# Closing layer 0's rounds with 32x32 block turns, and measuring half of the features inside layer 1's block

## The chip, the cores and the metric

The kernel runs on one core of a Trainium2 chip. The metric is the time of one execution on the device in microseconds. The core has five engines that run side by side, each with its own queue of instructions: TensorE (PE, with its weight load as PEld), VectorE (DVE), ScalarE (ACT), GpSimd (POOL) and SyncE (SP, which issues DMAs). They are ordered by semaphores alone. TensorE's clock has two levels, 1.2 and 2.4 GHz; the profile gives the granted clock as a share of the upper one.

## The reference

The input is x (2048 nodes x 256 features) and an adjacency matrix (2048 x 2048). Four layers follow each other, each of the form x = layernorm(x + layer(x)):

- Layer 0: attention with 8 heads of 32 over the neighbours. For each head, scores q k^T / sqrt(32), masked by the adjacency, softmax, times v.
- Layer 1: a graph attention layer. Wh = x W^T; e = leaky_relu(s_dst + s_src), masked, softmax, times Wh, which gives h_prime (2048 x 256). Then each *feature* is normalised over the 2048 nodes: `gamma * (h_prime - mean) * rsqrt(var + eps) + beta`, and relu.
- Layer 2: the mean over at most the first 64 neighbours of each node (a cumulative count along the row says which are kept), two projections with leaky relu.
- Layer 3: the mean over all neighbours, projections, relu.

## The kernel before

The program is one function after another, each with a block in which the five engines have their own instruction lists; at the end of a block all engines meet. `attention` is layer 0 and prepares for the next. `general_attention` follows it: a slow, exact way that runs only if a flag `doubt` says that a softmax sum was too small; in this run it is skipped, but every engine loads the flag and branches there. `layer1` computes h_prime; another `general_attention` follows, then `tail`, with the feature norm, layers 2 and 3.

**Layer 0** (`attention`). The work is laid out transposed: for a block of 512 destination nodes and a group of 4 heads, 16 tiles of 128 source nodes are gone through in 8 steps of two tiles. That is a *round*; there are 8 rounds, 64 steps (`STEPS`). In step s and for head h, TensorE makes scores for 2 x 512 (`score`, L340 and the mask added by L344) into one of three PSUM buffers; ScalarE takes the exponential (L484) into `ex`; VectorE adds it to a running sum `esum` (L555). After every second step TensorE multiplies two steps' `ex` by v into `mixed_ps` (`mix`, L359), in the order scores of step s, then mix of s-2 and s-1. At a round's end VectorE halves the sum (`halve`, L561), and TensorE sums over the partitions with a matrix of ones (`total`, L378, in the last round L370), so that `total_ps` has, for each of 4 heads, 32 equal rows of 512 totals. In the first half (steps below 32) ScalarE also turns the raw adjacency of coming tiles into marks of 8 bits (`convert`, L450, two at the end of each even step), and SyncE loads the raw tiles two steps ahead (L207). On some steps ScalarE and VectorE split inputs into a high and a low part (L441, L503).

The round is closed by VectorE in the next round, by `keep(it, piece)`, one piece behind each of its sums in steps 1 to 3 of that round (after the loop, all pieces for the last round): piece 0 copies `mixed_ps` to `yT` (L569, then `stored`, for which the next `mix` waits); 1 takes the maximum of the totals and a tiny number (L572); 2 finds the smallest total (L575, L577); 3 to 6 take the reciprocal in four parts of 128 (L581); 7 multiplies `yT` by it (L585); 8 adds the residual (L589), which SyncE loads after the totals (L217). After the last round a small matmul (`count_fine`, L98) and L659 make `doubt`.

**Layer 1** (`layer1`). Head by head, VectorE and ScalarE make masks and TensorE multiplies (L997 and L1004) into 8 PSUM banks, `acc`: banks 0 to 3 for the first half of the nodes, 4 to 7 for the second. VectorE joins the pieces of a half (`join_pieces`, L1121) and weighs them (`finish`). In the last head's loop `divide` writes h_prime for heads 0 to 6 (L1139); `finish_last` does the last head. Behind the main loop TensorE begins layer 2's cumulative count in banks 0 to 3 (class `Cumulation`): per tile t of 128 sources, `up_to_source` (L1715), `compare` on ScalarE with a sigmoid (L1729), and `cumulate` (L1721), each in 4 pieces of 512. These pass a tile to and fro between TensorE and ScalarE. Tiles 0 and 1 (`AHEAD`) are done in this block, then L98 and L1157 make `doubt`.

**The tail** (`tail`). SyncE loads gamma and beta. TensorE turns the first 128 features (k = 0) of h_prime with 16 transposes into banks 4 to 7 (L1364); VectorE measures them (`feature_stats`, four L1515 and L1517); GpSimd takes the root (L1650, L1652); VectorE makes the factors (L1521, L1524, L1527); ScalarE applies them with a relu into `hpT`, in two halves (L1464). Then the same for k = 1, turned into the same banks. Meanwhile the comparison goes on: tile 2 stands ahead of the first application on ScalarE, tiles 3 to 5 behind it, then the second application; from tile 6 on each step s of the loop has one comparison beside back turns, layer norm and projections of layer 2.

The order of all this is written out by hand, in each engine's list. The lines that the change touches lie in `attention` (`keep`, `sum_weights`, the loops of ScalarE and VectorE), `general_attention`, `layer1` (`finish_last` and the ends of the lists) and `tail`.

## Time and profile before

| | |
|---|---|
| median of 3 runs | 869.05 us (868.21 to 869.98) |
| the profiled execution's own time | 870.34 us |
| its span, first to last instruction | 868.6 us |
| mean granted clock of TensorE | 0.988 |
| TensorE busy | 810.2 us (93%) |
| VectorE busy | 691.6 us (80%) |
| ScalarE busy | 568.3 us (65%) |
| GpSimd busy | 148.5 us (17%) |
| layer 0 (span time) | 0 to 409 us |
| layer 1 | 409 to 644 us |
| tail | 644 to 868.6 us |

Times of rows are microseconds from the span's start. TensorE's matmuls overlap, so a busy TensorE is not one at its peak; a group that is named with x16 is a run of 16 instructions, and its time goes from the first's start to the last's end. An arrow `<-` in brackets says what an engine had waited for before the row.

### The profile page before, as it was taken

To read this page: it belongs to the slowest core of one execution; us is meant where nothing else is said; L and a number is where in the kernel's file an instruction comes from. 1 tells how busy PE (TensorE), PEld (TensorE's weight loads), DVE (VectorE), ACT (ScalarE), POOL (GpSimd) and SP (SyncE) were. 2 spreads that over 40 slices of the span, in tenths; PEclk is the share of its full clock that TensorE was granted. 3 is DMA by queue.
4 is the path that set the end of the run, shared out by engine and by line. 5 is a ranking of instruction groups with operands and counts; after the bars stand their busy time and mean duration, and the time that the engine had idled before them with its cause. 6 is when DMAs were issued, how large, how long until landed. Compare 5 with 4: busy or idle time off the path is not lost. (4 is left out here: it accounts for less than half of the span.)

```text
span 868.6 us, 18889 instructions
## 1 busy us (share of the span) xinstructions
PE 810.2 (93%) x7820; PEld 507.0 (58%) x7820; DVE 691.6 (80%) x1053; ACT 568.3 (65%) x568; POOL 148.5 (17%) x287
## 2 busy tenths in 40 slices
PE   3899999999999999995869999999968999999997
PEld 1334444333444434342559999999943557777786
DVE  6686989899998989897789999999943585555444
ACT  6798989897777767672369999999848630111000
POOL 2511011753110010000420000000001352111122
PEclk9999999999999999998999999999999999999999
DMA  8965344393302020001221111111000000000011
GB/s 291 263 197 169 110 137 144 95 246 85 99 16 58 1 61 1 14 1 37 85 86 52 51 32 48 32 48 48 3 1 1 1 1 1 1 1 1 2 49 49
DMA packets 28615, 56.85 MB, mean 65 GB/s; under 512 B 5808, under 2 KB 10032, under 8 KB 27120
## 3 DMA queue, kind: packets, MB, share of 16 engines
q1 hardware_dynamic: 24400, 46.19, 17.2%
q0 software_dynamic: 4128, 9.44, 4.1%
q8 instruction: 62, 1.02, 0.5%
q14 instruction: 25, 0.20, 0.1%
HBM read 38.70 MB, written 2.23 MB: 47 GB/s over the span
## 5 line engine op out<-in xcount | busy, mean ns | idle before, releaser
L484 ACT ACTIVATE ex<-scores_ps,shift 128x1024 f32<-128x1024 f32 x256 | 262.4, 1129 | 77.7 <-PE scores_ps L344 69.9
L555 DVE TENSOR_TENSOR esum<-esum,ex 128x1024 f32<-128x1024 f32 x192 | 222.9, 1211 | 7.1 <-ACT ex L484 7.1
L340 PE MATMUL scores_ps<-qst,kst 128*128 128x512 f32 x512 | 201.3, 474 | 2.9 <-ACT ex L484 2.2
L997 PE MATMUL banks<-fx,pos 128*128 128x132 f16 x2048 | 160.3, 221 | 7.1 <-DVE pos L1174 6.8
L1267 ACT ACTIVATE steps<-a_all,big_b_head 128x2048 fp8e5<-128x2048 f32 x86 | 163.6, 1988 | 0.0
L344 PE MATMUL scores_ps<-edge,negI 128*128 128x512 fp8e5 x512 | 155.3, 385 | 0.0
L340 PEld LDWEIGHTS scores_ps<-qst,kst 128*128 128x128 f32 x512 | 89.8, 189 | 70.9 <-ACT ex L484 19.8
L997 PEld LDWEIGHTS banks<-fx,pos 128*128 128x128 fp8e5 x2048 | 121.3, 98 | 8.0 <-issue 6.5
L1004 PE MATMUL banks<-fm,edge 128*128 128x66 f16 x2048 | 104.1, 193 | 0.0
L1004 PEld LDWEIGHTS banks<-fm,edge 128*128 128x128 fp8e5 x2048 | 86.6, 98 | 0.0
L1174 DVE TENSOR_TENSOR pos<-steps,edge 128x1024 int32<-128x1024 int32 (+1 forms) x65 | 77.4, 1202 | 2.4 <-PE banks L997 2.2
L344 PEld LDWEIGHTS scores_ps<-edge,negI 128*128 128x128 bf16 x512 | 29.7, 99 | 70.1 <-issue 70.1
L555 DVE TENSOR_TENSOR esum<-ex 128x1024 f32<-128x1024 f32 x32 | 38.9, 1221 | 32.8 <-ACT ex L484 32.5
L1394 PE MATMUL banks<-w,xT_ring 128*128 128x512 f32 x128 | 60.4, 594 | 0.7 <-DVE own L1558 0.6
L359 PE MATMUL mixed_total_ps<-ex,cur 128*32 128x512 f32 x512 | 58.2, 595 | 0.0
L359 PE MATMUL mixed_total_ps<-ex,v 128*32 128x512 f32 x512 | 58.2, 595 | 0.0
L1407 PE MATMUL banks<-y_halves_second,edge 128*128 128x256 f16 x512 | 56.7, 273 | 0.5 <-DVE y_halves_second L1552 0.5
L1407 PEld LDWEIGHTS banks<-y_halves_second,edge 128*128 128x128 fp8e5 x512 | 50.0, 98 | 8.7 <-issue 2.3
L284 POOL DMA_DIRECT2D qst<-high_low x56 | 27.6, 503 | 159.7 <-PE scores_ps L344 138.8
L1407 PE MATMUL banks<-y_halves,kept_rest 128*128 128x256 f16 x448 | 52.0, 273 | 0.5 <-DVE y_halves L1552 0.5
L1164 DVE TENSOR_SCALAR steps<-a_all,negb 128x2048 fp8e5<-128x2048 f32 x40 | 50.5, 1281 | 0.6 <-DMA a_all<-score_rows_dram 0.6
L1477 ACT COPY xT_ring<-banks 128x256 f32<-128x256 f32 x32 | 11.9, 371 | 57.1 <-PE banks L1383 56.8
(210 smaller groups left out, 915.5 us busy)
## 6 DMA issues: line engine op xcount, KB each, us to landing
adj_raw<-in_adjT_dram SPq DMA_DIRECT2D x32, 512.0 KB, 5.5
a_all<-score_rows_dram SPq DMA_DIRECT2D x7, 1024.0 KB, 4.7
kst<-high_low SPq DMA_DIRECT2D x56, 64.0 KB, 4.5
kst<-high_low POOLq DMA_DIRECT2D x56, 64.0 KB, 5.0
qst<-high_low POOLq DMA_DIRECT2D x56, 64.0 KB, 2.2
qst<-high_low SPq DMA_DIRECT2D x56, 64.0 KB, 3.7
ex<-in_x2T_dram SPq DMA_DIRECT2D x2, 1024.0 KB, 6.9
ex<-in_xT_dram SPq DMA_DIRECT2D x2, 1024.0 KB, 8.9
```

What stands on the lines that cost most here:

```text
L340: nc.tensor.matmul(to, kst[:, h, jt * P:(jt + 1) * P], qst[:, it % 2, h, :], start=True, stop=False)
L344: last = nc.tensor.matmul(to, negI[:], edge[:, jt, columns(it % NC)], start=False, stop=True)
L359: last = nc.tensor.matmul(mixed_ps[h * DH:(h + 1) * DH, :], (v0, v1)[it // NC][:, jt, h * DH:(h + 1) * DH], ex[:, s % ER, h, t * CW:(t + 1 ...
L484: nc.scalar.activation(ex[:, s % ER, h, :], scores_ps[:, u % SR, :], ACT.Exp, bias=shift[:, it // NC * HG + h:it // NC * HG + h + 1], scal ...
L555: nc.vector.tensor_tensor(esum[:, h, :], other, ex[:, s % ER, h, :], ALU.add).then_inc(summed, 1)
L997: done = nc.tensor.matmul(place(half, i), pos[:, group_of(h, k, half) % GR, jt % GU, i * P:(i + 1) * P], fx[:, e, jt].rearrange("p k r c - ...
L1004: done = nc.tensor.matmul(place(half, i)[:, C:2 * C], edge[:, jt, at:at + P], fm[:, e, jt].rearrange("p r c -> p (r c)"), start=False, sto ...
L1164: nc.vector.tensor_scalar(steps[:, pair_of(h, k) % SLOTS, jt % GU, :], aall[:, h % 2, :], negb[:, jt, one(h)], MARK, ALU.is_gt, ALU.mult, ...
L1174: nc.vector.tensor_tensor(pos[:, group_of(h, k, half) % GR, first:end, :].bitcast(int32), steps[:, pair_of(h, k) % SLOTS, first:end, at].b ...
L1267: nc.scalar.activation(steps[:, pair_of(h, k) % SLOTS, jt % GU, :], aall[:, e, :], ACT.Relu, bias=bigh[:, e, jt:jt + 1], scale=BIG, satura ...
L1394: last = nc.tensor.matmul(proj_ps[:, t % 2, :], xT[:, t % 2, k, :], (w2, w3)[layer][:, k, :], start=(k == 0), stop=(k == KT - 1))
L1407: last = nc.tensor.matmul(nb_ps[:, t % 2, 0:D], which, halves[layer][:, jt, r, :], start=(jt == 0 and r == 0), stop=(jt == T - 1 and r == 1))
```

## The change

In **layer 0** `keep` becomes `close`, with 5 pieces in place of 9. The copy of `mixed_ps` goes to ScalarE (`keep_mixed`), in step 0 of the next round behind the fourth exponential and ahead of the conversions, where it waits for the round's last mix. The totals, 32 equal rows per head, are turned in 32x32 blocks by VectorE (piece 0), so that each partition has 16 distinct values in one column of each block; maximum, minimum and reciprocal run on these 16 (piece 1); a second turn of the 16, spread over 32 each, gives the rows back (piece 2). Pieces 3 and 4 are the multiplication and the residual.

In **layer 1** gamma and beta are loaded; TensorE turns the first half of the features (k = 0), which `divide` has finished, into banks 0 to 3 behind the main loop, the last bank first, and VectorE measures them in `finish_last`; the cumulative count moves to banks 4 to 7 and behind these turns, and waits for the second half's join as well. `count_fine` writes to a column of the last feature bank, behind the first tile's cumulation; that column's tile is turned once more at the end. The general way turns and measures them anew if it runs.

In the **tail** the first steps are now the root and the factors of k = 0. Tile 2's comparison stands behind the first application. The PSUM banks 0 to 3 and 4 to 7 change places.

```diff
@@ attention
-    PIECES = 4
+    CLOSING = 4
-        recip, res = half_sum[:, 0, :], half_sum[:, 1, :]
+        recip, res, turned = half_sum[:, 0, :], half_sum[:, 1, :], half_sum[:, 2, :]
+        compact = S.sb("distinct_sums", [P, CW // DH], fp32)
@@ sum_weights (tensor)
-                    pe.wait_ge(recip_step, (s // JP - 1) * (PIECES + 1) + 1)
+                    pe.wait_ge(recip_step, (s // JP - 1) * CLOSING + 1)
@@ scalar
+                def keep_mixed(it):
+                    act.wait_ge(mixed, (it + 1) * JP)
+                    nc.scalar.copy(yT[:, it // NC, columns(it % NC)], mixed_ps).then_inc(stored, 1)
...
+                        if jp == 0 and it and h == HG - 1:
+                            keep_mixed(it - 1)
...
+                keep_mixed(ROUNDS - 1)
@@ vector
-                def keep(it, piece):
...
+                def close(it, piece):
+                    g, at, done = it // NC, columns(it % NC), it * CLOSING
                     if piece == 0:
-                        dve.wait_ge(mixed, (it + 1) * JP)
-                        nc.vector.tensor_copy(yT[:, g, at], mixed_ps).then_inc(stored, 1)
+                        dve.wait_ge(totals, it + 1)
+                        nc.vector.transpose(turned, total_ps).then_inc(recip_step, 1)
                     elif piece == 1:
-                        dve.wait_ge(totals, it + 1)
-                        nc.vector.tensor_scalar(recip, total_ps, TRUST / 2, None, ALU.max).then_inc(recip_step, 1)
-                    elif piece == 2:
-                        dve.wait_ge(recip_step, it * (PIECES + 1) + 1)
-                        nc.vector.tensor_reduce(out=least[:], in_=recip, axis=AX.X, op=ALU.min).then_inc(lowest, 1)
+                        dve.wait_ge(recip_step, done + 1)
+                        nc.vector.tensor_scalar(compact[:], turned.rearrange("p (b r) -> p b r", r=DH)[:, :, 0], TRUST / 2, None,
+                                                ALU.max).then_inc(recip_step, 1)
+                        dve.wait_ge(recip_step, done + 2)
+                        nc.vector.tensor_reduce(out=least[:], in_=compact[:], axis=AX.X, op=ALU.min).then_inc(lowest, 1)
                         dve.wait_ge(lowest, it * 2 + 1)
                         nc.vector.tensor_tensor(low, least[:], low, ALU.min).then_inc(lowest, 1)
-                        dve.wait_ge(lowest, it * 2 + 2)
-                    elif piece < 3 + PIECES:
-                        part = slice((piece - 3) * CW // PIECES, (piece - 2) * CW // PIECES)
-                        nc.vector.reciprocal(recip[:, part], recip[:, part]).then_inc(recip_step, 1)
+                        nc.vector.reciprocal(compact[:], compact[:]).then_inc(recip_step, 1)
+                    elif piece == 2:
+                        dve.wait_ge(recip_step, done + 3)
+                        nc.vector.transpose(recip, compact[:].unsqueeze(2).broadcast_to([P, CW // DH, DH])).then_inc(recip_step, 1)
@@ general_attention, layer 1 only
+                    if layer:
+                        pe.wait_ge(result_ready, U)
+                        pe.wait_ge(returned, 16)
+                        for b in range(NC):
+                            feature.turn(0, b).then_inc(summed, 1)
@@ layer1
+        cum_ps = acc[:, NC:2 * NC, :]
                 sp.wait_ge(pair_landed, there)
+                feature.load(sp, gamma, beta)
@@ tensor
                 pe.wait_ge(evac, LAST * 2 + 1 + EV0)
+                pe.wait_ge(heads_made, 1)
+                for b in feature.order(0):
+                    feature.turn(0, b).then_inc(feature.turned, 1)
+                pe.wait_ge(evac, LAST * 2 + 2 + EV0)
                 pe.wait_ge(count.consts, 3)
                 for c in range(NC):
-                    count.up_to_source(acc, 0, c)
+                    count.up_to_source(cum_ps, 0, c)
                 for t in range(count.AHEAD):
-                    count.cumulate(pe, acc, t)
-                count_fine(pe, nc, fine_made, ones, fine, acc[:, 7, 0:1], counted)
+                    count.cumulate(pe, cum_ps, t)
+                    if t == 0:
+                        pe.wait_ge(feature.stats, 1)
+                        count_fine(pe, nc, fine_made, ones, fine, feature.ps[:, NC - 1, 0:1], counted)
+                pe.wait_ge(counted, 2)
+                feature.turn(0, NC - 1, 1)
@@ finish_last (vector)
                     nc.vector.tensor_scalar(fine[:], low, MARK * SURE, None, ALU.is_ge).then_inc(fine_made, 1)
+                    feature.take_stats(dve, 0)
@@ tail
-        turn_hp = ps[:, NC:2 * NC, :]
-        cum_ps = ps[:, 0:NC, :]
+        cum_ps = ps[:, NC:2 * NC, :]
@@ tensor
                 for b in range(NC):
-                    turn_features(0, b)
-                count.cumulate(pe, cum_ps, count.AHEAD)
-                for b in range(NC):
-                    turn_features(1, b)
-                for t in range(count.AHEAD + 1, LEAD):
+                    if b % 2 == 0:
+                        pe.wait_ge(applied, b // 2 + 1)
+                    feature.turn(1, b).then_inc(feature.turned, 1)
+                for t in range(count.AHEAD, LEAD):
                     count.cumulate(pe, cum_ps, t)
@@ scalar
-                count.compare(act, cum_ps, count.AHEAD)
                 for half in range(2):
                     apply(0, half)
-                for t in range(count.AHEAD + 1, LEAD):
+                for t in range(count.AHEAD, LEAD):
                     count.compare(act, cum_ps, t)
@@ vector
-                feature_stats(0)
-                dve.wait_ge(gb_landed, 16 * (1 + KT))
-                feature_factors(0)
-                feature_stats(1)
-                feature_factors(1)
+                feature.factors(dve, 0)
+                feature.take_stats(dve, 1)
+                feature.factors(dve, 1)
@@ new: class FeatureNorm (load, take_stats, find_root and factors as in the tail before)
+    def load(self, sp, gamma, beta):
+        sp.dma_start(self.gcol[:], gamma).then_inc(self.landed, 16)
+        for k in range(KT):
+            sp.dma_start(self.bcol[:, k:k + 1], beta[k * P:(k + 1) * P].rearrange("(p o) -> p o", o=1)
+                         ).then_inc(self.landed, 16)
+        sp.wait_ge(self.landed, 16 * (1 + KT))
+
+    def order(self, k):
+        return range(NC) if k else (NC - 1, *range(NC - 1))
+
+    def turn(self, k, b, count=NC):
+        for t in range(NC * b, NC * b + count):
+            last = self.nc.tensor.transpose(self.ps[:, b, t % NC * P:(t % NC + 1) * P],
+                                            self.hp[:, t, k * P:(k + 1) * P], self.ident[:])
+        return last
```

## Rows read from the trace of the kernel before

**Rows 1.** Busy time by stretch: PE, PEld, DVE, ACT, POOL, PEclk, DMA share, GB/s.

```profile
350.00:398.00 48.00, 47.22 (x289) 18.78 (x287) 44.52 (x49) 32.27 (x32) 0.00 (x0) 1.00 0.02 6
644.50:712.00 67.50, 60.38 (x270) 29.84 (x270) 39.38 (x115) 46.36 (x65) 22.55 (x45) 1.00 0.01 1
```

**Rows 2.** Timeline of ScalarE at round boundaries (start us, us, ...).

```profile
120.46 2.23 ACT L450 ACTIVATE edge<-adj_raw,twos 128x1024 fp8e5<-128x1024 int32 x2
124.42 8.14 ACT L484 ACTIVATE ex<-scores_ps,shift 128x1024 f32<-128x1024 f32 x8 [1.73 <-PE scores_ps L344]
...
357.87 8.15 ACT L484 ACTIVATE ex<-scores_ps,shift 128x1024 f32<-128x1024 f32 x8 [4.16 <-PE scores_ps L344]
```

**Rows 3.** Timeline of TensorE at the boundary of 124 us.

```profile
118.77 3.64 PE L359 MATMUL mixed_total_ps<-ex,cur 128*32 128x512 f32 x32
...
129.60 0.73 PE L340 MATMUL scores_ps<-qst,kst 128*128 128x512 f32 x2
```

**Rows 4.** Groups by line and form, 60 to 400 us; last, the waits.

```profile
L581 DVE RECIPROCAL half_sum<-half_sum 128x128 f32<-128x128 f32 x28 | 26.4, 942 | 0.0
...
L441 ACT CAST high_low<-natural 128x512 fp32r<-128x512 f32 x9 | 5.6, 620 | 0.0
L569 DVE COPY cur<-mixed_total_ps 128x512 f32<-128x512 f32 x8 | 5.5, 684 | 0.0
...
PE mixed_total_ps L378 <- DVE half_sum L561: 0.7, 3, 0.3
```

**Rows 5.** Timeline of layer 0's end; last, the DMA issues (KB, us to landing).

```profile
391.11 4.13 ACT L484 ACTIVATE ex<-scores_ps,shift 128x1024 f32<-128x1024 f32 x4 [2.93 <-PE scores_ps L344]
...
393.74 3.64 PE L359 MATMUL mixed_total_ps<-ex,v 128*32 128x512 f32 x32
...
398.80 1.92 PE L370 MATMUL mixed_total_ps<-esum,ones 128*32 128x512 f32 x16 [1.42 <-DVE esum L555]
...
402.51 3.38 DVE L581 RECIPROCAL half_sum<-half_sum 128x128 f32<-128x128 f32 x4
...
406.64 0.69 DVE L589 TENSOR_TENSOR cur<-cur,half_sum 128x512 f32<-128x512 f32 x1
...
half_sum<-in_xT_dram SPq DMA_DIRECT2D x1, 256.0 KB, 3.1
```

**Rows 6.** Timeline of the end of layer 1's block.

```profile
633.68 1.02 PE L1715 MATMUL banks<-edge,before_in_tile 128*128 128x512 fp8e5 x4
...
634.36 1.28 ACT L1729 ACT_TABLE_LOAD   x1 [8.53 <-PE banks L1715]
...
635.65 2.12 ACT L1729 ACTIVATE kept_head<-banks,limit 128x1024 fp8e5<-128x1024 f32 x2
...
640.39 1.11 ACT L1729 ACTIVATE kept_head<-banks,limit 128x1024 fp8e5<-128x1024 f32 x1 [0.59 <-PE banks L1715]
...
642.75 0.16 DVE L1157 TENSOR_SCALAR doubt<-banks 128x1 int32<-128x1 f32 x1 [4.78 <-PE banks L98]
```

**Rows 7.** Timeline of the tail's first 17 us.

```profile
644.56 1.94 PE L1364 MATMUL banks<-ident,cur 128*128 128x128 f32 x16 [1.85 <-PEq L696]
...
647.75 0.26 DVE L1517 BATCH_NORM_AGGREGATE feature_mean_var<-feature_stats 128x2 f32<-128x24 f32 x1
...
649.65 2.30 ACT L1464 ACTIVATE hp_turned<-banks,feature_scale_shift 128x1024 f32<-128x1024 f32 x2 [1.66 <-DVE feature_scale_shift L1527]
...
654.15 2.12 ACT L1729 ACTIVATE kept_rest<-banks,limit 128x1024 fp8e5<-128x1024 f32 x2 [0.18 <-PE banks L1715]
...
660.65 2.12 ACT L1729 ACTIVATE kept_rest<-banks,limit 128x1024 fp8e5<-128x1024 f32 x2
```

**Rows 8.** Busy time by stretch (columns as in rows 1), with the granted clock.

```profile
638.50:640.30 1.80, 1.80 (x6) 0.59 (x5) 0.00 (x0) 1.11 (x1) 0.00 (x0) 0.50 0.00 0
```

**Rows 9.** Timeline of ScalarE, the first table load.

```profile
0.80 1.28 ACT L441 ACT_TABLE_LOAD   x1 [0.80 <-PEq L1906]
5.67 0.62 ACT L441 CAST high_low<-ex 128x512 fp32r<-128x512 f32 x1 [3.59 <-DMA ex<-in_x2T_dram]
```

More of the change, by code:

```diff
@@ L640, in _ @@
                         piece = (jp - 1) * HG + h
-                        if it and 0 <= piece <= 4 + PIECES:
-                            keep(it - 1, piece)
+                        if it and 0 <= piece <= CLOSING:
+                            close(it - 1, piece)
                         if W_AT + 2 <= s < W_AT + 4:
@@ L807, in _ @@
                             nc.vector.tensor_tensor(to[:, g, :], to[:, g, :], (sc, pT)[g][:], ALU.add)
+                    else:
+                        dve.wait_ge(summed, U + NC)
+                        step = Chain(dve, chain, U * STEPS)
+                        for b in range(NC):
+                            step(nc.vector.bn_stats(feature.st[:, 0, b, :], feature.ps[:, b, :]))
+                        nc.vector.bn_aggr(feature.mv[:, 0, :], feature.st[:, 0].rearrange("p b s -> p (b s)"))
 def layer1(nc, S, w, ident, ones, mhalf, yT, x1, edge, wh1, score_rows, fac, efac, negb, bigb, sums, low, fine, doubt,
-           hp, pair, count, sources, ps):
+           hp, pair, count, sources, ps, feature, gamma, beta):
     TG = 4
@@ L1298, in _, with tail @@
                 for t in range(count.AHEAD):
-                    count.compare(act, acc, t)
-def tail(nc, S, gamma, beta, ident, ones, mhalf, hp, cur, edge, w2, bias2, w3, bias3, eps1, scale, count, ps, out):
+                    count.compare(act, cum_ps, t)
+def tail(nc, S, ident, ones, mhalf, hp, cur, edge, w2, bias2, w3, bias3, scale, count, ps, feature, out):
     xn = cur[:, :].rearrange("p (t d) -> p t d", d=D)
@@ L1348, in _ @@
             def _(sp):
-                sp.dma_start(gcol[:], gamma).then_inc(gb_landed, 16)
-                for k in range(KT):
-                    sp.dma_start(bcol[:, k:k + 1], beta[k * P:(k + 1) * P].rearrange("(p o) -> p o", o=1)
-                                 ).then_inc(gb_landed, 16)
                 for t in range(0, T, TD):
@@ L1359, in _ @@
             def _(pe):
-                def turn_features(k, b):
-                    if k:
-                        pe.wait_ge(applied, b // 2 + 1)
-                    for t in range(NC * b, NC * (b + 1)):
-                        last = nc.tensor.transpose(turn_hp[:, b, t % NC * P:(t % NC + 1) * P],
-                                                   hp[:, t, k * P:(k + 1) * P], ident[:])
-                    last.then_inc(hp_turned, 1)
                 def back(t):
@@ L1648, in _ @@
                 for k in range(KT):
[L1649 to L1652 removed]
+                    feature.find_root(pool, k)
                 def root(n):
@@ L1879, in gat_layer @@
         layer1(nc, S, w, ident, ones, mhalf, yT, x1, edge, wh1, score_rows, fac, efac, negb, bigb, sums, low[:, 1:2], fine,
-               doubt[:, 1:2], hp, pair, count, sources, banks)
-        general_attention(nc, S, 1, doubt[:, 1:2], ident, (score_rows, wh1), adj, scratch1, hp, banks)
+               doubt[:, 1:2], hp, pair, count, sources, banks, feature, gamma, beta)
+        general_attention(nc, S, 1, doubt[:, 1:2], ident, (score_rows, wh1), adj, scratch1, hp, banks, feature)
 def kernel(x, adj, L0_gnn_x2, L0_gnn_v, L1_gnn_W, L1_gnn_a, L1_gnn_gamma, L1_gnn_beta, L2_gnn_W_nb, L2_gnn_b_nb,
```

114 lines of the change are left out of this document (59 added, 55 removed).

## The prediction

> **What bounds the kernel now.** Start with the busy time by stretch: in the second half of layer 0 TensorE works 47.22 of 48 us, VectorE 44.52, ScalarE 32.27; in the tail's first 67.5 us TensorE has 60.38, VectorE only 39.38 [rows 1]. Work taken from VectorE is worth something only where TensorE waits for it. So read next, one engine at a time, the two places where the engines wait for each other: a round boundary of layer 0, and the two block ends (layer 0, layer 1) where everything drains. The list of waits in the stretch 60 to 398 us shows 0.7 us in all of TensorE waiting for VectorE's half sums [rows 4]: VectorE's reciprocals in the rounds are covered. ScalarE is not free in the first four rounds: it also converts adjacency tiles, and waits only 1.73 us at the boundary at 124.42, against 4.16 us in a late round [rows 2].
>
> **Layer 0, ScalarE takes the copy of the mixed values.** The copy waits for the last mixing matmul of the round, and behind it in ScalarE's queue stand two conversions (2.23 us) and the exponentials of the next step. The mixing of the boundary shown ends at 118.77 + 3.64 = 122.41 [rows 3]; the conversions ran meanwhile, from 120.46 [rows 2]. Now they come after: 122.41 + 0.05 of latency, a copy of 128x512 (as the cast of that shape, 0.62, of which 0.1 overlaps the next instruction [rows 4]) to 122.98, conversions to 125.1, where the next exponential began at 124.42 [rows 2]: 0.7 us late. Is there slack? TensorE's eighth score of the pair of steps starts at 129.60 [rows 3] and needs the fifth exponential, which ends at 124.42 + 5 x 1.02 = 129.5 (1.02 is 8.14 / 8 [rows 2]). No slack is left, so TensorE is shifted by the 0.7, for good. Conversions stand at three boundaries (steps 8, 16, 24): **+2.1 us**. Bounds: 0 if something absorbs it, 3 x 1.0. At the four later ones the copy lies in an idle time of 4.16 us [rows 2], from after the mixing on: free. The adjacency loads are issued 0.7 us later and still two steps ahead of use; I take nothing for them.
>
> **Layer 0, VectorE.** Per round go a copy, a maximum and a minimum over 512 (0.68 each) and four reciprocals of 0.94 [rows 4], 5.8 us in all; two turns and three operations on 16 elements come. The trace shows no turn on VectorE. The nearest row is the copy of the same 512 columns out of PSUM, 0.68 [rows 4], and I take that, since both stream the tile once; the ends are a free turn and the reciprocal's pace, 4 x 0.94 = 3.8. The Trainium skill, VectorE: DVE Perf Modes, The three transpose paths, gives 311 ns for a 128x128 bf16 turn; four of them would be an estimated 1.24 us, and the sum below would end 1.1 us higher (two turns). A small operation costs between 0.16 (one element [rows 6]) and 0.94; I take 0.2. So 2 x 0.68 + 3 x 0.2 = 2.0 us replace 5.8, and VectorE gains 3.8 per round. In the rounds that buys the 0.7 us of waits [rows 4]: **-0.7 us**.
>
> At the end of layer 0 it buys more. TensorE's mixing ends at 393.74 + 3.64 = 397.38, but the totals start at 398.80, 1.42 us late, behind VectorE's last sum [rows 5]. ScalarE had given the last exponential at 391.11 + 4.13 = 395.24 [rows 5], so the last sum could end at 395.24 + 1.2 = 396.4, before the mixing does. VectorE is late by its backlog of 2.3 us, and 3.8 removes it: **-1.4 us**. What is late next is the mixing. Then all of the closing work is bare: out go 3.38 us of reciprocals [rows 5] and two passes of 0.68 [rows 4], 4.7 in all, in come 2.0 and some issue gaps of 0.1: **-2.6 us**. Its last step is the residual sum at 406.64 [rows 5]; the residual is loaded after the totals, 3.1 us to landing [rows 5], and is needed about 3.2 us after them now. That just fits; what is saved beyond this would be lost to it. (The final copy on ScalarE lies beside the totals; its cover is their 1.92 us.)
>
> **End of layer 1.** TensorE's first cumulating matmuls start at 633.68 [rows 6], right behind the main loop. Now 16 turns stand before them; the same 16 took 1.94 us in the tail [rows 7]. The wait for the second half's pieces, joined in the meantime, adds none. ScalarE's table load and all that follows are that much later: **+1.9 us**. VectorE's statistics (at most the 3.4 us from 644.56 to their end at 648.01 [rows 7]) come while ScalarE and TensorE pass the tiles to and fro, ahead of doubt, for which VectorE had waited 4.78 us [rows 6]: free, and so is the retaken single turn (a sixteenth of 1.94). The three small loads of gamma and beta now stand on SyncE's queue, with a wait for their landing, ahead of head 1's row; even 3.1 us as for the residual [rows 5] each lies beside head 0, an eighth of the main loop: nothing. Dropping them from the tail brings nothing either, the factors came after them.
>
> **The tail.** From its first instruction at 644.56 to the comparison of tile 6 at 660.65 are 16.1 us [rows 7]. In it ScalarE had room: it loaded its table and compared tile 2 in the shadow of the first half's turns, statistics and root. Now the chain is: root and factors, 649.65 - (647.75 + 0.26) = 1.64 us; two applications, 2.2 (2.30 less overlap); comparisons of tiles 2 to 5 at 2.12 + 0.18 each, 9.2, less a last 0.18; two applications, 2.2 [rows 7]. That is 15.1. A table load comes on top. The tail's first activation is now a Relu and no longer a sigmoid, so the sigmoid's table load (1.28 us, and 0.01 after it the activation starts [rows 6]) comes behind the applications, unhidden. A load ahead of the Relu, if there is one, stands before that activation's wait, as the one at 0.80 does [rows 9], and is over within the 1.64. Sum 16.3: **+0.2 us**. So 3.4 us of turning and measuring leave the chain, and a comparison of 2.3 and a load of 1.28 enter it. The Trainium skill, ScalarE: Activation LUTs, What ACT_TABLE_LOAD costs, puts a switch at 2.66 us with its drain; by that the sum would be 1.4 higher.
>
> **Sum.** +2.1 - 0.7 - 1.4 - 2.6 + 1.9 + 0.2 = -0.5 us against the profiled execution, whose own time is 870.34, 1.3 above the median of 869.05. Applied to the median: 868.6. A measurement of this kernel can tell 0.2%, 1.7 us, from no change.
>
> **The rivals.** (a) *The boundaries cost nothing*: some slack takes up ScalarE's 0.7, three times; -2.6 us, **866.5**. For it: TensorE waits little there. Against: row 129.60 fits ScalarE to 0.1 us. Chance 0.15. (b) *The clock stays up at the end of layer 1*: behind an idle TensorE (from 634.70 until half of the first comparison was done, 635.65 + 1.06: 2.0 us [rows 6]), the granted clock was 0.50 [rows 8] (1.2 of 2.4 GHz), and from the table load's end at 635.64 to the last comparison's end at 641.50 went 5.86 us [rows 6], where the tail's pace, 2.30 + 2.12, would make it 4.42. If the turns ahead keep the clock up, -1.4 more: **867.1**, chance 0.15. (c) *Slower, the clock falls in the tail*: TensorE now rests from the end of layer 1's block until the first application has ended, 1.6 us between the blocks (642.91 to 644.56 [rows 6, 7]), 1.64 and half of 2.3, 4.4 in all, longer than the 2.0 us before the row of 0.50. The difference in (b), 1.4 us, is what one tile's matmuls at half rate cost. On the forecast's -0.5, it decides from two such tiles on: +2.8, **871.4**. For: that row. Against: the fall comes not after every rest (1.85 us before 644.56 left the turns at full pace [rows 7]), and half rate over the turns alone is partly covered by the table load. Chance 0.15. (d) *A turn costs two passes*, 2 x 0.68, one to fill and one to empty its block, between the bounds: +1.4, **870.0**; or the table load holds ScalarE for two of its rows, 1.3 more, against [rows 6], which show 0.01 behind it: 869.9. Together 0.08. The two estimates from the Trainium skill above, each cited there with its page, come to about these. (e) *VectorE's backlog doesn't go*, so that the change does not do what it says at the end: the 1.4 stays, **870.0**, chance 0.05. The forecast itself, 868.6, has the remaining 0.42.
>
> **How the numbers follow.** Forecast, (d) and (e) lie within 0.2% of 869.05: 0.55. Faster: (a), (b) 0.30, the likelier small misses of the forecast on that side counted in them. Slower: (c), 0.15. The range runs from just below (a) up to (c) with two tiles, and leaves out three tiles, a turn at the reciprocal's pace, and (a) with (b): 866.0 to 871.4.
>
> **What would show it.** In the changed profile: a copy on ScalarE before the conversions at 124 us and the exponential after them 0.7 us later, the eighth score with it; the totals at layer 0's end starting with the mixing's end, and 2.7 us less from there to the last sum; the turn's row at 0.7 us; the first cumulating matmul 1.9 us behind the main loop; in the tail a table load between application and comparison, and 16.3 us to the comparison of tile 6. The prediction is wrong if the conversions stay in the mixing's shadow, if a turn takes over 1.3 us, or if the tail's granted clock is 0.5 over more than one tile.

## Result, and the profile after

| | before | after |
|---|---|---|
| median of the runs made together | 869.0 us (866.8 to 869.98, 5 runs) | 865.03 us (864.0 to 866.28, 5 runs) |
| ratio, 95% interval | | 0.9957 [0.9943, 0.9972] |
| the profiled execution's own time | 870.34 us | 866.28 us |
| its span, mean granted clock | 868.6 us, 0.988 | 864.4 us, 0.985 |

The kernel is faster by 4.0 us, 0.43%. The prediction said 868.6, from 866.0 to 871.4: too little gain, and the result lies below its range. Busy time of the changed kernel, from its page:

```profile
PE 813.0 (94%) x7821; PEld 510.5 (59%) x7821; DVE 665.1 (77%) x1037; ACT 574.2 (66%) x577; POOL 132.3 (15%) x287
```

VectorE has lost 26.5 us. The second half of layer 0, to be set beside [rows 1] (PE, PEld, DVE, ACT, POOL, clock, DMA share, GB/s):

```profile
350.00:398.00 48.00, 47.26 (x298) 18.76 (x296) 39.23 (x45) 31.98 (x33) 0.00 (x0) 1.00 0.02 6
```

TensorE is as busy there as before, with VectorE 5.3 us lighter. The gain is not in these shares, but in single waits. Layer 0 as the changed kernel's timeline has it, first ScalarE and TensorE at the boundary of [rows 2, 3]:

```profile
122.09 0.59 ACT L456 COPY cur<-mixed_total_ps 128x512 f32<-128x512 f32 x1 [1.85 <-PE mixed_total_ps L360]
122.58 2.19 ACT L451 ACTIVATE edge<-adj_raw,twos 128x1024 fp8e5<-128x1024 int32 x2
124.67 2.11 ACT L489 ACTIVATE ex<-scores_ps,shift 128x1024 f32<-128x1024 f32 x2
...
118.39 3.64 PE L360 MATMUL mixed_total_ps<-ex,cur 128*32 128x512 f32 x32
121.84 1.04 PE L379 MATMUL mixed_total_ps<-half_sum,ones 128*32 128x512 f32 x8
```

The copy waits for the mixing, the conversions come behind it, and the exponential follows at 124.67 with no idle time, 6.28 us after the mixing's start; in [rows 2, 3] it was 124.42 - 118.77 = 5.65. So each of the three boundaries costs 0.62. VectorE's closing work in the next steps:

```profile
126.94 0.71 DVE L576 STREAM_TRANSPOSE half_sum<-mixed_total_ps 128x512 f32<-128x512 f32 x1
127.58 1.18 DVE L563 TENSOR_TENSOR esum<-ex 128x1024 f32<-128x1024 f32 x1
128.68 0.17 DVE L579 TENSOR_SCALAR distinct_sums<-half_sum 128x16 f32<-128x16 f32 x1
128.88 0.17 DVE L582 TENSOR_REDUCE least_sum<-distinct_sums 128x1 f32<-128x16 f32 x1
129.09 0.16 DVE L584 TENSOR_TENSOR lowest_sums<-least_sum,lowest_sums 128x1 f32<-128x1 f32 x1
129.16 0.25 DVE L585 RECIPROCAL distinct_sums<-distinct_sums 128x16 f32<-128x16 f32 x1
129.32 1.16 DVE L563 TENSOR_TENSOR esum<-ex 128x1024 f32<-128x1024 f32 x1
130.40 0.70 DVE L588 STREAM_TRANSPOSE half_sum<-distinct_sums 128x512 f32<-128x512 f32 x1
```

A turn of 128x512 f32 takes 0.71, whether it reads PSUM or spreads 16 columns: the duration of the copy it was priced by. By the Trainium skill, VectorE: DVE Perf Modes, The three transpose paths, it would have been an estimated 1.24; these rows decide. The end of layer 0, TensorE and then VectorE, to be set beside [rows 5]:

```profile
391.91 3.64 PE L360 MATMUL mixed_total_ps<-ex,v 128*32 128x512 f32 x32
395.37 1.90 PE L371 MATMUL mixed_total_ps<-esum,ones 128*32 128x512 f32 x16
...
403.19 0.66 PE L966 MATMUL banks<-ident,cur 128*128 128x128 f32 x2 [3.91 <-PEq L706]
...
397.33 0.72 DVE L576 STREAM_TRANSPOSE half_sum<-mixed_total_ps 128x512 f32<-128x512 f32 x1 [2.28 <-PE mixed_total_ps L371]
...
400.56 0.69 DVE L596 TENSOR_TENSOR cur<-cur,half_sum 128x512 f32<-128x512 f32 x1 [0.20 <-DMA half_sum<-in_xT_dram]
```

The totals now follow the mixing at once, and from their start to the last sum are 5.19 us, where there were 7.84. The end of layer 1 and the tail's start, TensorE and then ScalarE, beside [rows 6, 7]:

```profile
627.84 1.94 PE L1748 MATMUL banks<-ident,cur 128*128 128x128 f32 x16
629.61 1.03 PE L1703 MATMUL banks<-edge,before_in_tile 128*128 128x512 fp8e5 x4
...
642.98 3.53 PE L1748 MATMUL banks<-ident,cur 128*128 128x128 f32 x16 [4.35 <-ACT hp_turned L1476]
...
630.29 1.28 ACT L1717 ACT_TABLE_LOAD   x1 [10.31 <-PE banks L1703]
...
640.21 1.28 ACT L1476 ACT_TABLE_LOAD   x1 [2.79 <-PEq L706]
641.72 2.30 ACT L1476 ACTIVATE hp_turned<-banks,feature_scale_shift 128x1024 f32<-128x1024 f32 x2 [0.22 <-DVE feature_scale_shift L1772]
644.04 1.28 ACT L1717 ACT_TABLE_LOAD   x1
645.33 2.12 ACT L1717 ACTIVATE kept_rest<-banks,limit 128x1024 fp8e5<-128x1024 f32 x2
...
656.46 2.13 ACT L1717 ACTIVATE kept_rest<-banks,limit 128x1024 fp8e5<-128x1024 f32 x2
```

The turns put the first cumulating matmul 1.77 us behind the main loop; the tail has two table loads, the first hidden behind the root, the second not. TensorE's clock fell to its lower level over the turns of the second half of the features (busy time by stretch, columns as in [rows 1]; the clock is the third number from the end):

```profile
642.98:646.50 3.52, 3.52 (x16) 3.13 (x17) 2.10 (x3) 3.49 (x4) 0.00 (x0) 0.53 0.02 5
```

Behind an idle time of 4.35 they took 3.53 us, not 2.19 as in kernels where they follow 1.82 of idle. The cover is the table load and tile 2's comparison: tile 3's comparison waited only 0.21 for TensorE.

### The profile page after: what moved, and what is told of

It reads as the page before. It is cut to its first block and busy times, and to the rows that moved or that the text cites. A ratio compares the mean times of both kernels' runs of the same rounds, so it can differ in the third digit from the quotient of the medians.

```text
span 864.4 us, 18885 instructions
## 1 busy us (share of the span) xinstructions
PE 813.0 (94%) x7821; PEld 510.5 (59%) x7821; DVE 665.1 (77%) x1037; ACT 574.2 (66%) x577; POOL 132.3 (15%) x287
## 3 DMA queue, kind: packets, MB, share of 16 engines
q0 software_dynamic: 4128, 9.44, 4.4%
q8 instruction: 63, 1.03, 0.5%
## 5 line engine op out<-in xcount | busy, mean ns | idle before, releaser
L563 DVE TENSOR_TENSOR esum<-esum,ex 128x1024 f32<-128x1024 f32 x192 | 223.3, 1219 | 18.1 <-ACT ex L489 17.9
L360 PE MATMUL mixed_total_ps<-ex,cur 128*32 128x512 f32 x512 | 58.2, 595 | 0.0
L360 PE MATMUL mixed_total_ps<-ex,v 128*32 128x512 f32 x512 | 58.2, 595 | 0.0
```

Of the source, the lines that this page charges most:

```text
L360: last = nc.tensor.matmul(mixed_ps[h * DH:(h + 1) * DH, :], (v0, v1)[it // NC][:, jt, h * DH:(h + 1) * DH], ex[:, s % ER, h, t * CW:(t + 1 ...
L563: nc.vector.tensor_tensor(esum[:, h, :], other, ex[:, s % ER, h, :], ALU.add).then_inc(summed, 1)
```

## Where the 4.2 us of the span come from

I followed the start of each mixing (L359, L360 after) through layer 0 in both traces, then the marks of the rows above. Change against the trace of before, step by step:

| step | predicted | measured |
|---|---|---|
| up to the second mixing | 0 | -1.03 |
| three boundaries with conversions | +2.1 | +1.86 |
| step 28, within a round | 0 | +0.13 |
| rounds from step 32 on: half sums | -0.7 | -0.49 -0.32 -0.44 -0.36 = -1.61 |
| weights' sums (L386) in step 38 | 0 | -1.29 |
| totals behind the last mixing | -1.4 | 5.06 - 3.46 = -1.60 |
| closing work to the last sum | -2.6 | -2.65 |
| to layer 1's first matmul | 0 | -0.24 |
| layer 1 | 0 | +0.48 |
| turns ahead of the count | +1.9 | +1.77 |
| comparisons of tiles 0, 1 and block end | 0 | -0.30 |
| tail up to tile 6 | +0.2 | +0.18 |

With 0.1 of rounding along the mixings this is the -4.2 of the span; behind tile 6 both kernels take 207.9 us. Three rows make the miss: the start, the half sums and the weights' sums. The +0.13 is not the copy's: at 182.22 a conversion had waited 0.98 for its adjacency tile's DMA, and experiment 1's trace, with the same list, has 0.00 there. Layer 1's loop took from 223.3 to 224.9 us over the traces of this study, in no order of the edits, so +0.48 is scatter.

The weights' sums stand in the trace of before, TensorE and VectorE, though I hadn't read them:

```profile
246.88 3.64 PE L359 MATMUL mixed_total_ps<-ex,v 128*32 128x512 f32 x32
251.75 1.19 PE L386 MATMUL mixed_total_ps<-w,ones 128*128 128x272 f32 x4 [1.23 <-DVE w L601]
...
250.15 1.22 DVE L555 TENSOR_TENSOR esum<-esum,ex 128x1024 f32<-128x1024 f32 x1
251.28 0.41 DVE L601 TENSOR_REDUCE w<-adj_raw 128x8 f32<-128x256 f32 x1
```

and the changed kernel's:

```profile
247.41 3.64 PE L360 MATMUL mixed_total_ps<-ex,v 128*32 128x512 f32 x32
250.98 1.18 PE L387 MATMUL mixed_total_ps<-w,ones 128*128 128x272 f32 x4
...
248.26 0.41 DVE L608 TENSOR_REDUCE w<-adj_raw 128x8 f32<-128x256 f32 x1
```

VectorE, without its reciprocals, ends the last reduction 3 us earlier, and TensorE goes from the mixing to the sums with no wait. The same list of waits from which [rows 4] took 0.7 has these lines for the kernel before (us in total, times, longest):

```profile
PEld mixed_total_ps L378 <- DVE half_sum L561: 4.9, 5, 1.2
PEld mixed_total_ps L386 <- DVE w L601: 2.1, 1, 2.1
PE mixed_total_ps L386 <- DVE w L601: 1.2, 1, 1.2
```

The list of the changed kernel has none of them. The half sums show why the idle time of PE is too small a price for such a wait:

```profile
355.65 1.06 PE L378 MATMUL mixed_total_ps<-half_sum,ones 128*32 128x512 f32 x8 [0.16 <-DVE half_sum L561]
```

The mixing before it had started at 351.85, 3.80 earlier; where nothing waits the distance is 121.84 - 118.39 = 3.45, less than the mixing's own 3.64, since the next group overlaps it. So a row of 0.16 idle costs 0.35, and the ones of 0.29 and 0.24 (at 215.16 and 310.09) cost 0.49 and 0.44. The totals at 263.93 show no idle time at all, and cost 0.32.

## The experiments

All ratios are against the kernel before, run beside each group of kernels: 869.08 us for experiments 1 to 4, 868.39 for 5 to 8 (made on another chip), 868.94 for 9 to 11. The changed kernel's own 865.03 stood beside 869.0. So kernels of different groups are compared by their ratios, of which 0.001 is 0.9 us.

**1. Layer 0's part alone**: `attention` of the changed kernel, all else of the one before.

> Only the change in layer 0, the feature norm as before. Theory A (the traces laid side by side): layer 0 gave 6.3 us up to the start of layer 1, of which 1.0 stood already before the first round was closed and may be scatter; the features cost 2.1. Then this alone is 5.3 to 6.3 us below before, some 863. Theory B (the prediction's own sum for layer 0, -2.6, with the rest scatter): 2.6 below, 866.4. Theory C (the gain comes from the features after all): within 1 us of before.

Measured: 863.52 us (861.94 to 865.59), ratio 0.9932 [0.9917, 0.9948]. Its steps in layer 0 are those of the changed kernel, save the 0.13. This part alone brings more than the whole change.

**2. The features' part alone**: `attention` of before, the rest changed.

> Only the features turned and measured in layer 1's block, layer 0 as before. Theory A: the turns put the first cumulating matmul 1.8 us behind the main loop and the tail takes 0.2 longer to the comparison of tile 6: 2 us above before, 871. Theory C: 2 us or more below before.

Measured: 871.51 us (868.79 to 873.48), ratio 1.002 [1.0006, 1.0034]. In its trace no step of layer 0 differs from before by over 0.02, except +0.28 at the first mixing and -0.57 at the second, of which experiment 11 tells. The two parts give, by their ratios, -5.9 and +1.7 us, -4.2 in all, against 4.0 measured for the whole change. The prediction had -2.6 and +2.1. So the miss lies in layer 0; the features part costs what it was said to cost.

**3. The copy behind the conversions**, in the changed kernel:

```diff
@@ scalar, attention
-                        if jp == 0 and it and h == HG - 1:
-                            keep_mixed(it - 1)
...
                             convert(s + AHEAD + 1)
+                        if jp == 0 and it and h == HG - 1:
+                            keep_mixed(it - 1)
```

> The changed kernel, with ScalarE's copy of the mixed values behind the two conversions and not ahead of them. Theory A: each of the three early boundaries is 0.62 us late through the order alone, so 1.9 us below the changed kernel, 863.1, and the exponential at 124 us starts 0.87 behind its score's wait as before. Rival: the copy itself is the 0.6, wherever it stands: no change against the changed kernel.

Measured: 863.6 us (861.47 to 865.19), ratio 0.9933 [0.9918, 0.9948]. The three steps of +0.62 are gone (within 0.01), and all others of layer 0 stay; at the boundary the exponential now waits 1.25 for its score, so the copy lies in idle time. The medians differ by 1.4 of the 1.9 that these steps show. The end of layer 1 came out 1.4 shorter in this trace than in the changed kernel's, though nothing was changed there; experiment 6 tells why.

**4. VectorE's load put back**: four reciprocals of 128x128 in each of rounds 1 to 7, on a slice that nobody reads meanwhile (the last halving of the next round waits for them).

```diff
@@ vector, attention
+                        if it and CLOSING < piece <= CLOSING + 4:
+                            n = piece - CLOSING - 1
+                            part = half_sum[:, 3, n * P:(n + 1) * P]
+                            nc.vector.reciprocal(part, part).then_inc(filled, 1)
```

> The changed kernel with four reciprocals of 128x128 put back on VectorE in each of rounds 1 to 7, on half sums that nothing reads any more, so that VectorE is as loaded as before but the closing at layer 0's end stays short. Theory A (VectorE's backlog was what TensorE waited for, at five boundaries, at the weights' column sums and at the last totals): 1.6 + 1.3 + 1.5 = 4.4 us come back, some 869.4. Rival (the prediction: 0.7 + 1.4): 2.1 come back, 867.1.

Measured: 867.9 us (867.09 to 870.3), ratio 0.9989 [0.9976, 1.0001]: 2.9 us of the gain are gone, between the rival's 2.1 and theory A's 4.4. Waits for VectorE are back (list of waits, as above; last, TensorE's timeline at layer 0's end):

```profile
PEld mixed_total_ps L379 <- DVE half_sum L573: 3.7, 5, 1.0
PEld mixed_total_ps L387 <- DVE w L612: 1.8, 1, 1.8
PE mixed_total_ps L387 <- DVE w L612: 0.9, 1, 0.9
...
398.11 1.92 PE L371 MATMUL mixed_total_ps<-esum,ones 128*32 128x512 f32 x16 [1.06 <-DVE esum L565]
```

The totals stand 398.11 - 393.40 = 4.71 behind the last mixing's start, so 1.25 of their 1.60 are back. The step at the weights' sums is -0.36, not -1.29: 0.93 back. The half sums' are -0.30, 0, -0.35, -0.36, so only 0.6 of their 1.6 are back, most of it at one place. That makes 2.8 us, the 2.9 of the medians. What stayed away fits the load: VectorE still has 0.3 us less to do in a round than before (from the first sum of round 4 to its closing work's end 236.24 - 219.18 = 17.06, before 235.87 - 218.53 = 17.34), and 0.30 to 0.36 are missing at five of the six places. So the reciprocals' load brings back most of the waits at the weights' sums and at the last totals, one half sum's in full and another's in part. That the other two belong to it as well is argued from the size of this rest, and from their going with the turns in experiments 1 and 9.

**5. A sigmoid of one column ahead of the tail's first application**, so that the sigmoid's table is loaded in the shadow of the root.

```diff
@@ scalar, tail
+                nc.scalar.activation(warm[:], mhalf[:, 0:1], ACT.Sigmoid)
                 for half in range(2):
                     apply(0, half)
```

> The changed kernel with one sigmoid of a single column ahead of the first application in the tail. Theory A: the sigmoid's table (which serves the relu too) is then loaded in the 1.6 us in which ScalarE waits for the factors, and the second load behind the applications (1.28 us, at 644.04) is gone: 1.2 us less from the tail's first instruction to the comparison of tile 6, 863.8. Rival: TensorE's turns at half clock (3.53 us, to 646.5) end the wait for tile 2's cumulation whatever ScalarE does: then only some 0.2 us of it are gained.

Measured: 865.59 us (864.01 to 867.0), ratio 0.9966 [0.9955, 0.9978]: no gain. Its tail, ScalarE and TensorE:

```profile
641.87 2.31 ACT L1477 ACTIVATE hp_turned<-banks,feature_scale_shift 128x1024 f32<-128x1024 f32 x2
644.06 2.12 ACT L1719 ACTIVATE kept_rest<-banks,limit 128x1024 fp8e5<-128x1024 f32 x2
647.72 2.12 ACT L1719 ACTIVATE kept_rest<-banks,limit 128x1024 fp8e5<-128x1024 f32 x2 [1.54 <-PE banks L1705]
...
643.12 3.16 PE L1750 MATMUL banks<-ident,cur 128*128 128x128 f32 x16 [4.36 <-ACT hp_turned L1477]
646.08 0.63 PE L1711 MATMUL banks<-edge,after_in_tile 128*128 128x512 fp8e5 x1
```

The second load is gone and tile 2's comparison comes 1.4 us earlier, counted from the tail's start, but tile 2's cumulation stands behind the turns at the lower clock, and tile 3 waits 1.54 for it. Load and turns are two covers of nearly the same length; taking away one shows the other. The tail's 16.2 us stay (640.36 to 656.53).

**6. Tile 0's count ahead of the turns**: the count back in banks 0 to 3, the features in 4 to 7.

```diff
@@ tensor, layer1
+                pe.wait_ge(count.consts, 3)
+                for c in range(NC):
+                    count.up_to_source(cum_ps, 0, c)
                 pe.wait_ge(heads_made, 1)
+                pe.wait_ge(evac, LAST * 2 + 2 + EV0)
                 for b in feature.order(0):
                     feature.turn(0, b).then_inc(feature.turned, 1)
-                pe.wait_ge(evac, LAST * 2 + 2 + EV0)
-                pe.wait_ge(count.consts, 3)
-                for c in range(NC):
-                    count.up_to_source(cum_ps, 0, c)
```

> The changed kernel with tile 0's first cumulating matmuls ahead of the feature turns at the end of layer 1's block (the count in banks 0 to 3 and the features in banks 4 to 7, as the tail had them before). Theory A: the 1.8 us by which the turns delayed the count come back, and since TensorE is busy with the turns while ScalarE loads its table and compares tile 0, the granted clock stays up there, which gives another 1.4: 2.5 to 3.2 us less, 862. Rival (the clock falls all the same): 1.4 to 1.8 less, 863.4.

Measured: 862.54 us (862.32 to 863.27), ratio 0.9937 [0.9924, 0.995]. By the ratios that is 1.7 us below the changed kernel (0.9957), which does not exclude the rival. TensorE, and ScalarE's second comparison:

```profile
627.56 1.02 PE L1703 MATMUL banks<-edge,before_in_tile 128*128 128x512 fp8e5 x4
629.16 1.94 PE L1748 MATMUL banks<-ident,cur 128*128 128x128 f32 x16 [0.58 <-DVE part L1152]
630.93 0.38 PE L1709 MATMUL banks<-edge,after_in_tile 128*128 128x512 fp8e5 x1
...
632.06 2.12 ACT L1717 ACTIVATE kept_head<-banks,limit 128x1024 fp8e5<-128x1024 f32 x2 [0.41 <-PE banks L1703]
```

The turns now fill the time in which TensorE had waited for ScalarE, its idle time there shrinks to 0.58, and the cumulating matmuls behind it take 0.38, the pace of the upper clock, not 0.63. From the end of the main loop to the tail's start are 636.97 - 627.56 = 9.41 us, where the changed kernel has 640.21 - 627.84 = 12.37 and the one before 644.58 - 633.68 = 10.90. It is tempting to read this as the turns' 1.77 back and 1.2 of what the lower clock costs. But in the trace of experiment 9, whose list at this place is the changed kernel's, the same matmuls ran at the upper clock too, behind the same idle time of 2.11 (first the changed kernel, then experiment 9):

```profile
632.75 0.47 PE L1709 MATMUL banks<-edge,after_in_tile 128*128 128x512 fp8e5 x1 [2.11 <-ACT kept_head L1717]
633.02 0.63 PE L1703 MATMUL banks<-edge,before_in_tile 128*128 128x512 fp8e5 x1
...
630.50 0.39 PE L1708 MATMUL banks<-edge,after_in_tile 128*128 128x512 fp8e5 x1 [2.11 <-ACT kept_head L1716]
630.72 0.38 PE L1702 MATMUL banks<-edge,before_in_tile 128*128 128x512 fp8e5 x1
```

All traces side by side, from the main loop's end to the tail's start in us:

| order at the end of layer 1 | the clock fell there | the clock stayed up |
|---|---|---|
| count, no turns | 10.90, 10.47, 10.76 (before, experiments 11, 7) | 9.45 (experiment 1) |
| turns, then count | 12.37, 12.50, 12.19 (changed, experiments 2, 5) | 10.96, 10.96, 10.98 (experiments 3, 4, 9) |
| tile 0's count, then turns | | 9.41, 9.42, 9.44 (experiments 6, 8, 10) |

At a like clock the turns ahead of the count cost 1.5 to 1.6 us, and the turns behind tile 0's first matmuls cost nothing. The clock costs another 1.0 to 1.5, and it differs between traces of one and the same list. That it stayed up in the three traces of the last row may be the order's doing or chance; three traces don't show it. In the tail the clock falls in this order too, and its 16.2 us to tile 6 stay (653.19 - 636.97).

**7. Layer 0's part with the copy behind the conversions**, nothing of the features (edits 1 and 3).

> Only the change in layer 0, with the copy behind the conversions. Theory A: the two effects add: 1.5 to 1.9 us less than the layer 0 part alone (863.5), some 861.8.

Measured: 860.27 us (859.67 to 861.03), ratio 0.991 [0.9896, 0.9923]. By the ratios it is 1.9 us below experiment 1 (0.9932), as theory A had it, and 4.1 below the changed kernel. It is the lowest median of all, but experiments 8 and 10 can't be told from it.

**8. All three edits** (3, 5 and 6) in the changed kernel.

> The changed kernel with all three edits: the copy behind the conversions, the sigmoid first, tile 0's matmuls ahead of the turns. Theory A: they add: 865.0 - 1.5 - 1.2 - 2.8 = 859.5, below the layer 0 part alone with its copy behind, so that the feature part, put this way, is a gain. Rival (the features are no gain in any order): 861.8 or above.

Measured: 860.7 us (859.62 to 862.32), ratio 0.9912 [0.9898, 0.9925]. Measuring the features early, in this order, is no loss any more, and no gain over experiment 7 either. From the main loop's end to the tail's start it takes 9.42 us against experiment 7's 10.76, but that is the clock: experiment 1, with experiment 7's list there, took 9.45 with the clock up. The trace was taken of the slowest of the five executions (862.32): TensorE's clock falls over the tail's turns, tile 3's comparison waits 2.41 for TensorE, and the clock falls a second time behind tile 6:

```profile
652.00:655.80 3.80, 3.61 (x10) 1.49 (x11) 0.00 (x0) 2.25 (x3) 0.58 (x2) 0.55 0.00 0
```

In experiment 7's trace the clock of this stretch is 1.00.

**9. The copy left on VectorE**, the turns kept.

```diff
@@ vector, attention, close, piece 0
+                        dve.wait_ge(mixed, (it + 1) * JP)
+                        nc.vector.tensor_copy(yT[:, g, at], mixed_ps).then_inc(stored, 1)
                         dve.wait_ge(totals, it + 1)
                         nc.vector.transpose(turned, total_ps).then_inc(recip_step, 1)
```

> The changed kernel, in which VectorE keeps the copy of the mixed values (ahead of its wait for the totals, in the same piece), so that only the turns distinguish its rounds from before. Theory A (the gain of the rounds comes from the turns, and the copy on ScalarE brought nothing but the three boundaries): the steps of +0.62 us at steps 8, 16 and 24 are gone; VectorE has 0.68 more in each round, still 3.4 less than before, which keeps most of the steps of 0.3 to 0.5 at steps 32 to 56 and at least 0.7 of the 1.29 at the weights' sums; at the end of layer 0 the totals start no more than 0.3 later than in the changed kernel. Median 863 to 864.5, near that of the version with the copy behind the conversions (863.6). Rival B (VectorE stands just at a threshold, and the copy is what brought it under): most of the steps at 32 to 56 and at the weights' sums go, as with the four reciprocals put back: 866 to 868.

Measured: 862.7 us (862.13 to 865.43), ratio 0.9936 [0.992, 0.9952]. The steps of +0.62 are gone. Those of the half sums are -0.50, -0.31, -0.45, -0.36, that at the weights -1.30, as in the changed kernel, and the totals stand 3.46 behind the last mixing's start, as there. Step 28 has +0.31, behind a conversion that waited 1.16 for its adjacency tile's DMA. So the turns bring the whole gain of the rounds; the move of the copy to ScalarE brings none, and in the changed kernel's place costs its three boundaries. Behind the conversions (experiment 3) it costs and brings nothing that can be told.

**10. Experiment 8 without the early sigmoid.**

> The changed kernel with the copy behind the conversions and tile 0's count ahead of the turns, without the early sigmoid: the version with all three edits less one. If the early sigmoid brings nothing also where the clock stays up at the end of layer 1 (theory A: what the tail waits for is TensorE's turns at half rate and the cumulation behind them), the median is within 0.5 of 860.7. Sum of the single edits: 865.0 - 1.4 (copy) - 2.5 (count first) = 861.1. Rival B: in this order ScalarE's second table load is the bound, and leaving the sigmoid out costs 1.0 to 1.3: 861.7 to 862. Rival C: the sigmoid in front moved work against TensorE's clock, and without it the time is below 860.2.

Measured: 861.18 us (860.39 to 861.69), ratio 0.9912 [0.9898, 0.9926], within 0.5 of experiment 8: the early sigmoid brings nothing here either. In this trace the second fall is absent, and from the main loop's end to the last instruction are 233.6 us against 234.8 in experiment 7's. That is no gain of the features: experiment 1's trace, with the features as before and the clock up at the end of layer 1, takes 233.5, and the ratios, 0.9912 and 0.991, show none. If the features part can win something on top of experiment 7, it is less than these runs can tell.

**11. The kernel before, once more, for its trace.**

> The kernel before, once more, for its trace alone. Theory A (its profiled execution was some 1 us late in its first 12 us by scatter of the first loads, not by anything that the change touches): the first scores and the second mix come 0.5 to 1.1 us earlier than in the trace shown, and all steps between the mixes after it are within 0.1 of that trace: three waits for half sums, 1.23 at the weights' sums, totals 1.4 behind the mixing, half rate in the same places. Rival B: the start comes out as in the trace shown, and the other kernels are early through their own lists. Profiled time 867.5 to 870.5.

Measured: 869.59 us, span 867.9. Its first mixings come 0.62 and 1.19 us earlier than in the trace shown, though the first scores start within 0.01 of it, and every step after them up to the end of layer 0 is within 0.03. All eleven other traces are early at the second mixing too, by 0.29 to 1.46: the -1.03 of the table's first line belongs to that one execution. The end of layer 1 took 10.47 us, not 10.90, and the tail was different too, in TensorE's first turns:

```profile
642.66 3.56 PE L1364 MATMUL banks<-ident,cur 128*128 128x128 f32 x16 [1.83 <-PEq L696]
```

Behind 1.83 of idle they ran at the lower clock, where the trace of before shows 1.94 us behind 1.85 [rows 7]. The first application came 6.21 us after the tail's start, not 5.07: 1.1 us lost, about as much as was won at the start.

## Why the prediction was wrong

**The step that failed** is this one: "In the rounds that buys the 0.7 us of waits [rows 4]: -0.7 us". It is wrong twice. The waits for the half sums were worth 1.6, in four steps that go with the turns in experiments 1 and 9 as well (experiment 4 brings back one in full and one in part), since each costs the lost overlap on top of its idle time and one shows no idle at all; the line of the weight load, 4.9 over five waits, said that there was more. And the wait of 1.23 for the weights' column sums, one line further in the same list, is missing: 1.3 more, of which experiment 4 brings back 0.9. So "VectorE's reciprocals in the rounds are covered" was false. I had searched the list for one cause (half sums) where the question was all waits for VectorE. Together that is 2.2 of the 3.6 us by which the median was missed.

**The start**, 1.0 of the profiled execution, was its scatter, as experiment 11 shows, and falsifies no term. Without it the steps of the table come to -3.2, within the interval of the medians (-5.0 to -2.4). Of the 1.4 us that are left of the miss, some 0.5 is spread over small differences in the traces; layer 1 and the two block ends among them (-0.24, +0.48, -0.30) nearly cancel. The last two are no larger than what traces of unchanged stretches differ by. The first is not scatter: eight of the nine traces with the copy on ScalarE have 2.63 or 2.64 us there, the three with the old closing 2.85 to 2.87; its cause stays open. The other 0.8 or so lies between the steps of the two traces and the medians, and stays open; the clock at the end of layer 1, which differs between executions, is one candidate.

**The boundaries** held: +0.62 each, predicted 0.7; experiment 3 takes them away. Rival (a), that slack takes them up, is refuted. **The end of layer 0** held in both terms, -1.6 for -1.4 and -2.65 for -2.6, with the turn at 0.71 as priced. The residual became the last to arrive, by 0.20, as the prediction's "just fits" had it. **The end of layer 1** held, +1.77 for +1.9 (1.5 to 1.6 up to the tail's start at a like clock). **The tail** held, +0.18 for +0.2, with a table load between application and comparison and the first one hidden. By the Trainium skill, ScalarE: Activation LUTs, What ACT_TABLE_LOAD costs, a switch would be 2.66 us with its drain; here the comparison starts 1.29 after the load's start, so that sum would have been 1.4 too high.

**Rival (c)**, the clock falling in the tail, came true as a fact and, in this trace, not as a price: the turns at 642.98 ran at the lower level, but beside the table load, so they cost nothing; experiment 5 shows them as the next limit. In experiment 3's trace the same list of the tail took 16.80 us, not 16.25, with 0.76 of waiting ahead of tile 3's comparison, so there the fall cost 0.55. Rival (b) did not come about in this trace (tile 1's cumulation still ran at the lower clock, its matmuls 0.63 each), but it did in those of experiments 3, 4 and 9, whose list is the same there, and in experiment 1's, which has no turns there. What the prediction took for a property of the kernel is one of the execution. Rivals (d) and (e) are refuted by the turn's row and by the totals' start. None of the three signs that the prediction named for its being wrong came about: they watched the costs, and none watched the size of the gain in the rounds.

## What to carry to other kernels

When work leaves an engine, list every wait for that engine, in the list of matmuls and in that of weight loads, and price each by the distance between the starts of the two groups against a place where nothing waits, not by the idle time alone. Work moved to another engine's queue goes behind what others wait for: the same copy cost 0.6 us per boundary ahead of two conversions and nothing behind them. A step moved forward into an idle time is free only if it stands inside it; the same 16 turns cost 1.5 to 1.8 us ahead of the matmuls that feed ScalarE and nothing behind them. Before a clock that stayed up in one trace is credited to an edit, look at the same place in every other trace whose list there is unchanged.

## What the runs showed of the hardware

- A 32x32 block turn on VectorE, 128x512 f32, takes 0.71 us, from PSUM or from a 16-column operand spread by 32, against 0.68 for a plain copy of that size. A reciprocal of 128x128 takes 0.94, one of 128x16 takes 0.25.
- ScalarE's table load for the tail's first application stood ahead of that activation's wait, though the function is a Relu, and was followed by another for the sigmoid, 1.28 us each. With a sigmoid as the first function there was one load only.
- TensorE's clock isn't the same in every execution of one kernel: the same 16 turns behind 1.83 and 1.85 us of idle took 3.56 and 1.94 us. Behind 4.35 to 4.37 of idle they took from 3.46 to 3.68, and 3.16 in one kernel. At the end of layer 1, behind the same 2.11 of idle in the same list, the cumulating matmuls took 0.63 in one trace and 0.38 in another, which made the stretch 12.37 and 10.98. A difference of 1 us or so at such a place in two single traces needs a second trace before it is put to an edit.
